# Attention with every second quad masked by VectorE and shifted by GpSimd, scores four quads ahead

## The reference

```python
def step(carry, inputs):                       # one chunk here, as S = CHUNK = 128
    scores = jnp.einsum('bhqd,bhkd->bhqk', q, kj) * SCALE
    causal = j0 + k_off > q_idx
    scores = jnp.where(causal[None, None], -jnp.inf, scores)
    chunk_max = scores.max(axis=-1, keepdims=True)
    new_m = jnp.maximum(m, chunk_max)
    exp_c = jnp.exp(scores - new_m)
    new_s = s * exp_old + exp_c.sum(axis=-1, keepdims=True)
    out = out * (s / new_s) * exp_old + jnp.einsum('bhqk,bhkd->bhqd', exp_c / new_s, vj)
x = x + jnp.tanh(g_xattn[1]) * _L1_xattn_ref(_layernorm(x, axis=-1), ctx_2048, ctx_2048)
```

## Time and profile before

| what | value |
|---|---|
| time, median of 3 runs (lowest to highest) | 874.42 us (873.53 to 876.92) |
| the profiled execution's own time | 873.9 us |
| its span, first to last instruction | 872.1 us |
| attention stage in that span | about 368 to 482 us |
| PE busy over the span | 856.3 us, 98% |
| DVE, ACT, POOL busy over the span | 585.3, 522.1, 133.5 us |

### The profile page before, as it was taken

One profiled execution on the slowest core, in us unless ns is written; L12 is line 12 of the kernel. 1 busy time (PEld: TensorE's weight loads), 2 busy tenths in 40 slices (PEclk: granted clock), 3 DMA queues, 4 the chain that ended last, 5 costly groups with the idle time before them and its releaser, 6 DMA issues.

```text
span 872.1 us, 13796 instructions
## 1 busy us (share of the span) xinstructions
PE 856.3 (98%) x4700; PEld 706.2 (81%) x4700; DVE 585.3 (67%) x1225; ACT 522.1 (60%) x900; POOL 133.5 (15%) x125
## 2 busy tenths in 40 slices
PE   7999999999999999999999999999999999999998
PEld 7999887888788888877777788887888888888886
DVE  4998754565735665599999776569655566666664
ACT  3334434343553444456786867777777877777774
POOL 7996100000111310013223300000000000000000
PEclk9999999999999999999999999999999999999999
DMA  8230232334366833056765053444444344444433
GB/s 285 111 121 32 84 104 95 107 97 139 110 204 209 245 110 98 27 153 186 207 211 164 8 188 125 145 141 137 138 134 124 119 145 145 145 145 145 145 121 108
DMA packets 77348, 119.04 MB, mean 136 GB/s; under 512 B 9888, under 2 KB 36800, under 8 KB 76896
## 3 DMA queue, kind: packets, MB, share of 16 engines
q1 hardware_dynamic: 77072, 118.08, 43.2%
q10 hardware_dynamic: 208, 0.09, 0.0%
HBM read 96.81 MB, written 12.94 MB: 126 GB/s over the span
## 4 chain that ended last, share of the span: by engine, by line
PE 86%; DVE 8%; POOL 2%; issue 2%; ACT 1%; DMA 1%; DVEq 0%; SPq 0%; POOLq 0%; ACTq 0%
PE bank L714 39%; PE bank L750 29%; PE bank L1616 3%; PE bank L1627 2%; PE bank L1238 2%; PE bank L1239 2%; PE bank L1607 1%; PE bank L1257 1%; PE bank L1236 1%; PE bank L1601 1%; DVE max L1811 1%; DVE y L1817 1%; PE bank L383 1%; PE bank L1636 1%; PE bank L365 1%
## 5 line engine op out<-in xcount | busy, mean ns | idle before, releaser
L496 ACT ACTIVATE y_hi<-y 128x512 fp32r<-128x512 f32 x200 | 124.1, 621 | 79.9 <-DVE y L596 79.1
L610 DVE TENSOR_TENSOR y<-y,gate_rows 128x512 f32<-128x512 f32 x124 | 85.7, 691 | 116.9 <-ACT y L485 115.1
L750 PE MATMUL bank<-y_hi,w_hi 128*128 128x512 f32 x400 | 156.9, 392 | 1.4 <-DVE y_lo L330 1.3
L750 PE MATMUL bank<-y_hi,w_lo 128*128 128x512 f32 x400 | 155.8, 389 | 0.0
L750 PE MATMUL bank<-y_lo,w_hi 128*128 128x512 f32 x400 | 155.7, 389 | 0.0
L330 DVE TENSOR_TENSOR y_lo<-y,y_hi 128x512 fp32r<-128x512 f32 x196 | 134.3, 686 | 30.0 <-ACT y_hi L496 29.6
L479 ACT ACTIVATE activated<-bank 128x512 f32<-128x512 f32 x136 | 81.2, 597 | 77.1 <-PE bank L714 69.6
L714 PE MATMUL bank<-x_hi_first,w_hi 128*128 128x512 f32 x264 | 105.0, 398 | 0.7 <-DVE w_lo L325 0.7
L714 PE MATMUL bank<-x_hi_last,w_hi 128*128 128x512 f32 x264 | 104.0, 394 | 0.0
L714 PE MATMUL bank<-x_hi_first,w_lo 128*128 128x512 f32 x264 | 103.0, 390 | 0.0
L714 PE MATMUL bank<-x_hi_last,w_lo 128*128 128x512 f32 x264 | 102.9, 390 | 0.0
(11 more groups left out here) (160 smaller groups left out, 1321.1 us busy)
## 6 DMA issues: line engine op xcount, KB each, us to landing
gate_rows<-gates SPq DMA_DIRECT2D x156, 256.0 KB, 3.6
w_raw<-in_wu SPq DMA_DIRECT2D x68, 256.0 KB, 2.6
w_raw<-in_wu SPq DMA_DIRECT2D x32, 384.0 KB, 3.3
k_parts<-xn_split SPq DMA_DIRECT2D x64, 128.0 KB, 2.0
k_blocks<-k_parts SPq DMA_DIRECT2D x64, 128.0 KB, 2.9
q_split_t<-xn_split SPq DMA_DIRECT2D x64, 128.0 KB, 2.6
v_slot<-in_v_rows SPq DMA_DIRECT2D x16, 256.0 KB, 3.7
ctx_windows<-in_ctx_win SPq DMA_DIRECT2D x3, 1024.0 KB, 13.0
```

The costliest lines, as they stand in the source:

```text
L496: act.activation(mem.yhi[:, K % S, :], mem.y[:, K % S, :], ACT.Copy).then_inc(s_yh, 1)
L610: dve.tensor_tensor(mem.y[:, K % S, :], mem.y[:, K % S, :], gate, ALU.mult).then_inc(s_yd, 1)
L750: last = pe.matmul(acc(s)[:, c, :], w_[:, Nu % S, wc], y_[:, K % S, :], start=(n == 0 and m == 0), stop=(n == U - 1 and m == 2), skip_grou ...
```

## The change

For odd quads from 3 to 55 (`by_pool`), PE leaves out the mask's matmul; DVE adds the mask as it writes the scores from PSUM to SBUF (`masked`), takes the maximum from SBUF (`masked_maxima`), and POOL subtracts it in place (`shifted_by_pool`). `turned` waits for POOL in these quads (semaphore `c_shifted_by_pool`). PE makes scores four quads ahead instead of two. ACT normalizes and rounds a query in the step t = 0 instead of t = 1 and 2; POOL makes its rest, and the residual of two batches before, at t = 1; `query_turned`, `query_copy`, `inverse`, `scaled` and `moments` move by a step or more; some copies of the next layer's router move by one quad.

```diff
+            def by_pool(n):
+                return n % 2 == 1 and SR <= n < NQ - 8
...
-                pe.matmul(s_bank(n), identb[:], causal[:].rearrange("p h k -> p (h k)"), start=True, stop=False)
+                if not by_pool(n):
+                    pe.matmul(s_bank(n), identb[:], causal[:].rearrange("p h k -> p (h k)"), start=True, stop=False)
...
             def turned(pe, n):
-                pe.wait_ge(s_d, n + 1)
+                if by_pool(n):
+                    pe.wait_ge(s_ps, by_pool_to(n))
+                else:
+                    pe.wait_ge(s_d, n + 1)
...
             def c_gpsimd(pool):
+                def shifted_by_pool(n):
+                    pool.wait_ge(s_m, n + 1)
+                    pool.tensor_tensor(Ds[:, n % DR], Ds[:, n % DR],
+                                       nmax[:, n % DR, :].unsqueeze(2).broadcast_to((P, 4, P)), ALU.subtract).then_inc(s_ps, 1)
+
                 for n in range(NQ):
                     b, t = n // 4, n % 4
-                    if t == 2 and b + 3 < NB:
+                    if by_pool(n):
+                        shifted_by_pool(n)
+                    if t == 1 and b + 3 < NB:
                         query_lo(pool, b + 3)
-                    if t == 3 and b > 0:
+                    if t == 1 and b > 1:
+                        residual(pool, b - 2)
+                    if n == NQ - 1:
                         residual(pool, b - 1)
...
             def c_tensor(pe):
+                def scores_at(n):
+                    if n == 0:
+                        return (2, 3)
+                    if n == 3:
+                        return (6, 7)
+                    return tuple(m for m in (n + 3 if n < 3 else n + 4,) if m < NQ)
...
-                    if n + 2 < NQ:
-                        scores(pe, n + 2)
+                    for m in scores_at(n):
+                        scores(pe, m)
...
-                    if n == 52:
+                    if n == 51:
                         pe.wait_ge(f1.s_l, 2)
...
-                    if t == 0 and b > 0 and b + 2 < NB:
-                        query_turned(pe, b + 2)
+                    if t == 3 and b + 3 < NB:
+                        query_turned(pe, b + 3)
...
-                    if t == 1 and b > 0 and b + 2 < NB:
+                    if t == 0 and b > 0 and b + 2 < NB:
                         query_copy(act, b + 2)
...
-                    if t == 1 and b + 3 < NB:
+                    if t == 0 and b + 3 < NB:
                         query_normed(act, b + 3)
-                    if t == 2 and b + 3 < NB:
                         query_hi(act, b + 3)
...
+                def masked(n):
+                    if n == SR:
+                        dve.wait_ge(s_cc, 32)
+                    dve.wait_ge(s_s, n + 1)
+                    if n >= DR:
+                        dve.wait_ge(s_tt, n - DR + 1)
+                    dve.tensor_tensor(Ds[:, n % DR], s_bank(n).rearrange("p (h k) -> p h k", k=P), causal[:], ALU.add).then_inc(s_d, 1)
+
+                def masked_maxima(n):
+                    dve.wait_ge(s_d, n + 1)
+                    dve.tensor_reduce(nmax[:, n % DR, :], Ds[:, n % DR], AX_X, ALU.max).then_inc(s_m, 1)
...
-                    if n + 1 < NQ:
+                    if by_pool(n + 1):
+                        masked(n + 1)
+                    elif n + 1 < NQ:
                         maxima(n + 1)
-                    if t == 3 and b > 0:
+                    if t == 0 and b > 1:
+                        inverse(dve, b - 2)
+                    if n == NQ - 1:
                         inverse(dve, b - 1)
-                    if t == 1 and b > 1:
+                    if t == 2 and b > 1:
                         moments(dve, b - 2)
-                    if n + 1 < NQ:
+                    if by_pool(n + 1):
+                        masked_maxima(n + 1)
+                    elif n + 1 < NQ:
                         shifted(n + 1)
...
-                    if n in (51, 59):
+                    if n in (52, 60):
                         f1.x_lo(dve, b // 2 - 6, 1, x_bank)
-                    if n in (55, 63):
-                        f1.logits_copy(dve, b // 2 - 6, x_bank)
-                    if t == 3 and b > 0:
+                    if n in (56, 63):
+                        f1.logits_copy(dve, 0 if n == 56 else 1, x_bank)
+                    if t == 0 and b > 1:
+                        scaled(dve, b - 2)
+                    if n == NQ - 1:
                         scaled(dve, b - 1)
```

More of the change, by code:

```diff
@@ L1572, in attention @@
             s_gf = sem("c_gate_column")
+            s_ps = sem("c_shifted_by_pool")
             s_m = sem("c_max")
@@ L1585, in s_bank, with by_pool_to @@
                 return bk(n % SR)
+            def by_pool(n):
+                return n % 2 == 1 and SR <= n < NQ - 8
+            def by_pool_to(n):
+                return sum(1 for m in range(n + 1) if by_pool(m))
             o_bank, row_bank = bk(6), bk(7)
@@ L1607, in scores @@
                     last = pe.matmul(s_bank(n)[:, a * 2 * P:(a + 1) * 2 * P], Q1[:, b % 2, a, t, :], blocks[:, :, a, :],
-                                     start=False, stop=(a == 1))
+                                     start=by_pool(n), stop=(by_pool(n) or a == 1))
                 last.then_inc(s_s, 1)
             def turned(pe, n):
-                pe.wait_ge(s_d, n + 1)
+                if by_pool(n):
+                    pe.wait_ge(s_ps, by_pool_to(n))
+                else:
+                    pe.wait_ge(s_d, n + 1)
                 if n >= 2:
@@ L1742, in c_tensor @@
                         f0.out_turned(pe, 1, 1, 1, row_bank)
-                    if n == 4:
+                    if n == 3:
                         pe.wait_ge(f0.s_xa, 7)
-                    if n == 52:
+                    if n == 51:
                         pe.wait_ge(f1.s_l, 2)
@@ L1810, in maxima @@
                     dve.wait_ge(s_s, n + 1)
+                    if n >= DR and by_pool(n - DR):
+                        dve.wait_ge(s_ps, by_pool_to(n - DR))
                     dve.tensor_reduce(nmax[:, n % DR, :], s_bank(n).rearrange("p (h k) -> p h k", k=P), AX_X, ALU.max).then_inc(s_m, 1)
@@ L1839, in c_vector @@
                         negated(dve, "c", 1)
-                    if n in (50, 58):
+                    if n in (51, 59):
                         f1.x_lo(dve, b // 2 - 6, 0, row_bank)
-                    if n in (51, 59):
+                    if n in (52, 60):
                         f1.x_lo(dve, b // 2 - 6, 1, x_bank)
-                    if n in (55, 63):
-                        f1.logits_copy(dve, b // 2 - 6, x_bank)
-                    if t == 3 and b > 0:
+                    if n in (56, 63):
[3 more added lines that the diff above has]
+                    if n == NQ - 1:
                         scaled(dve, b - 1)
```

## The result

The changed kernel takes 912.58 us (median of 4 runs, 909.04 to 914.96); beside it the kernel before took 875.67. The ratio is 1.041 (95% interval 1.038 to 1.044): slower, as forecast, by 37 us where 26 were forecast. All rows of after are from its profiled execution of 909.04 us (span 907.2).

The account below looks back on a forecast made before the run. The prediction took PE, busy 98% of the span, as the bound; 1.1 + 24.0 + 1.3 = +26.4 us on 873.9 gave 900.3, median 901 us; own range 894 to 909, wider range 886 to 916.

Parts of the forecast that it names:

- the ring: Attention, once a batch: waits from PE through ACT, POOL and DVE back to PE, 8.69 us against 6.35.
- the signs that were listed as "wrong": Attention: PE waits before quads 4b+1, for scores or query transfers; slow POOL subtraction; clock under 1.00; or 109 us without POOL waits.
- Quad 7: Stretch up to quad 7: PE starts it at 384.74 instead of 383.63, after DVE's maximum and POOL's subtraction, +1.1 us.
- The turn: Transposes of quad 4b-1 to those of 4b+3: 8.69 us, 11 times from quad 7 to 51, 95.6 us against 73.83.
- The extras: Quads 7 to 51: 2.2 us more for POOL's rstd in batch 3 and ACT's small rows in batches 10 to 12.
- the look-ahead: Scores made four quads ahead: their wait for DVE is met when PE gets there, costed at nothing.
- the tail: Behind quad 51: three things stand later, estimated 1.5 us, less 0.2 for one saved mask, +1.3.
- The clock: Rival: PE returns from each gap at 1.2 GHz, 34 us more over 11 turns, 935 us; chance 0.10.
- the stall that I had named: Quad 58: DVE's bn_stats waits for a residual behind POOL's weight split; part of the 1.5 us estimate.
- POOL keeps up: Rival in the attention: PE stays the bound and each saved mask counts, 869 us; chance 0.08.
- Half the ring: Rival: bn_stats and maximum lie off the ring, 7.56 us a turn, 12.4 us less, 889 us; chance 0.10.
- The claimed gain of 5.4 us from the masks: Attention on PE: 27 quads lose the mask's matmul at 0.20 us each, the whole gain to be had.

Follow-up runs that it names:

- the kernel with the filler: Changed kernel plus nine matmuls with unused results on PE before the transposes of quad 4b+3, in batches 2 to 11: 904.84 us, ratio 1.0326.
- moments late: Changed kernel with DVE's bn_stats of batch b-2 moved behind the maximum of quad 4b+3: 887.7 us, ratio 1.0129.
- The moves alone: Changed kernel with no subtraction by POOL and every mask on PE, all moved steps and scores four ahead kept: 924.29 us, ratio 1.0559.
- three ahead: Changed kernel with POOL's low part and DVE's bn_stats behind the subtraction, scores three quads ahead, POOL's weight splits two quads later: 874.65 us, ratio 0.9986.
- copy behind the query: Changed kernel with ACT's two query steps ahead of the output's copy instead of behind it: 890.14 us, ratio 1.0144.

## Why the prediction was right, and what it missed

The mechanism was right: ten turns end with PE waiting 1.46 to 2.14 us for POOL, where 2 to 3 were forecast, and moving one instruction of the ring opens it. Two of the signs that were listed as "wrong" showed as well, a granted clock under 1.00 (0.92 in the stage) and PE's waits for scores; both are accounted for below. The working gave 900.3 us for the profiled execution; it took 909.04. The 8.7 us between them, by the terms of the sum:

- *Quad 7*, +1.1 us (384.74), came at 384.81, +1.18.
- *The turn*, 8.69 us: ten of its eleven terms are within 0.04 us of the rows. The mis-sized one is POOL's subtraction, taken at 1.28 us from two full operands; the maximum from SBUF came close to its 0.68.

```profile
L1720 POOL TENSOR_TENSOR y<-y,max x27: 1038/1040/1042, 375.8 to 494.6; 128x512 f32<-128x512 f32 x27
...
L1858 DVE TENSOR_REDUCE max<-y x27: 629/668/687, 375.0 to 493.9; 128x4 f32<-128x512 f32 x27
```

  11 turns of 8.42 are 92.6 us, 3.0 less than predicted. On the maximum, the Trainium skill's "VectorE: DVE Perf Modes" ("The TRN2 errata") would have 0.06 us less from SBUF than from PSUM; the medians differ by 0.012, so the rows are nearer to no difference.
- *The extras*, 2.2 us, are 5.3 (five turns, in which the clock was low, are taken from the kernel with the filler): 1.2 instead of 0.2 in batch 10, 2.2 instead of 0.6 in batch 12, and 0.5 more in small pieces elsewhere. In batch 10, DVE's variances for the next layer (L145 to L161, from 456.25) stand ahead of quad 40's maximum and subtraction; PE's scores of quad 43 need the bank that this subtraction frees, and start 1.42 us after quad 39's transposes instead of 0.41. That is the look-ahead, which the prediction put at nothing. (POOL's rstd is in the same place, but is done before the subtraction behind it, which waits 0.71 us for DVE's maximum.) Batch 12's turn ends with PE waiting 3.16 us for DVE's x_lo: the prediction put such late steps into the tail alone. PE's waits at L1615 (scores that have no mask's matmul ahead of them) from 368 to 520 us, and the two rows:

```profile
PE bank L1615 <- DVE y L1845: 3.0, 5, 1.1
...
458.92 0.80 PE L1615 MATMUL bank<-k_blocks,q_split_t 128*128 128x256 f32 x2 [0.76 <-DVE y L1845]
...
488.77 0.85 PE L1647 MATMUL bank<-ident,o_t 128*128 128x128 f32 x4 [3.16 <-DVE x_lo_first L375]
```

- *The clock*, a rival with a chance of its own and not a term of the sum, did fall, in five of the eleven turns: 9.67, 9.97, 9.87, 11.37 and 11.65 us against 8.41, 8.77, 8.42, 9.59 and 10.63 with the filler, 6.7 us together (a little more, since in the last of these the clock was 0.91 with the filler, too). The rival's full price, 34 us, was far off, since PE came back slow only after some of the gaps.
- *The tail* (quads 51 to 63, by PE's starts), +1.3, was 24.59 - 21.97 = +2.6: 0.8 in quads 51 to 55, where the clock was low once more (0.83), 2.7 in quads 55 to 59, and 0.9 less behind. The 2.7 are the stall that I had named: POOL splits a weight ahead of the residual, DVE's bn_stats waits for it, and PE's scores wait for DVE.

```profile
504.47 0.43 DVE L1690 BATCH_NORM_STATS2 stats<-X 128x6 f32<-128x256 f32 x1 [2.91 <-POOL X L1686]
...
505.54 0.39 PE L1609 MATMUL bank<-causal,identb 128*128 128x512 bf16 x1 [1.56 <-DVE y L1845]
```

That is -3.0 + 3.1 + 6.7 + 1.3, with 0.6 in the stretches before and behind. That the first two cancel is luck. The median lies 3.5 us above the profiled execution; the mean granted clock is 0.980 to 0.982 in the other runs and 0.986 in this one. The median of 912.58 us is above the forecast's own range (894 to 909); it is within 886 to 916 only because that was left open for a clock that falls in some turns, as it did.

Of the rivals, *POOL keeps up* falls with the waits. *Half the ring* falls as a forecast, but its step was sound: without bn_stats and the maximum a turn was to be 1.13 us shorter, and with the moments late it was 1.17 (8.42 to 7.25). That the total, 887.7 us, came so near to the 889 worked out is partly luck, since the clock came back as well. The claimed gain of 5.4 us from the masks was too high even for a ring that is open: DVE's own 6.0 us a batch end it then, so it went from 6.35 to 6.07 us, not to 5.95, and that only where nothing else disturbed it.

The step that failed in my reasoning, though not in the number, is the look-ahead: I costed it at nothing by DVE's distance in the ring, when what decides is which instruction frees the bank. It cost 1.0 us in batch 10 of the change, and 26 us in *The moves alone*.

## What to carry to other kernels

Before giving a step of the critical path to an idle engine, list what stands ahead of it in that engine's order and what those wait for: here 27 subtractions with time to spare on POOL came late because one waiting instruction stood ahead of every second one. Follow the waits back to the engine that you started from; if you arrive there within one batch, the loop's durations are the new batch time, and moving one waiting instruction behind the hand-over can open it. And read the second-fullest engine before counting a gain: with DVE over 90% busy the masks' 5.4 us were mostly not there to be had.

## What the hardware showed

- TensorE's granted clock fell to 0.50 (1.2 GHz) six times in the stage of after, as in the row 437.90:441.30: after five gaps of 2.01 to 2.14 us and one of 3.16. After two others, of 2.13 and 2.06 us (the one that ends at 411.15 and the first row of the turn above), it did not fall, nor after shorter ones. In other runs it also fell after shorter ones: at 403.94 after 1.60 us (moments late), at 383.79 after 1.65 (three ahead), and at 487.65 around 1.56 and 0.94 (copy behind the query), a pair that did no such thing behind 504 us in after. With gaps of about 0.6 and 0.7 us in every turn (copy behind the query) or 0.96 (moments late) it stayed at 1.00; with those of 2.3 to 2.5 us of the moves alone it averaged 0.83 from 400 to 480 us. The Trainium skill's "TensorE: Matmul & The Clock Gate" (Part 1) lets the clock fall after idleness; the traces agree that gaps go before the falls. Why only some gaps count wasn't settled here.
- A POOL subtraction of 128x512 with a broadcast maximum as its second operand, in place, took 1.04 us; its addition of two full operands of that size took 1.27. POOL's subtraction of two full operands into fp32r (`w_lo`, L325) took 1.28, so that it subtracts doesn't explain it alone; the broadcast operand may, which wasn't tried.
